# Graph-masked attention on one core: where the softmax probabilities are turned, and which queue places the head halves

## What is computed

```python
h = relu(layernorm(x))                        # x: (32, 256, 384) float32
q, k, v = h @ Wq + bq, h @ Wk + bk, h @ Wv + bv      # 6 heads of 64
scores = einsum('bhqd,bhkd->bhqk', q, k) / 8
bias = where(adj, 0.0, -9e15)[:, None]        # adj: (32, 256, 256) bool
probs = softmax(scores + bias, axis=-1)
ctx = einsum('bhqk,bhkd->bhqd', probs, v)     # back to (32, 256, 384)
out = x + (ctx @ Wf + bf)
```

## Time and profile before

| | us |
|---|---|
| median of three runs | 701.88 (701.35 to 702.62) |
| span of the profiled execution | 701.6 |
| TensorE busy | 677.3 |
| VectorE busy | 555.2 |
| ScalarE busy | 464.9 |
| GpSimd busy | 270.1 |

### The profile page before, as it was taken

How to read it: one execution, slowest core, us unless ns; L and a number is a source line. 1 busy time by engine, 2 the same in 40 slices (tenths; PEclk the granted TensorE clock), 3 DMA queues, 4 the chain that set the end, 5 groups by cost and what they waited for, 6 DMA issues and landing times.

```text
span 701.6 us, 21244 instructions
## 1 busy us (share of the span) xinstructions
PE 677.3 (97%) x7156; PEld 562.7 (80%) x7156; DVE 555.2 (79%) x1676; ACT 464.9 (66%) x972; POOL 270.1 (39%) x330
## 2 busy tenths in 40 slices
PE   7688999999999999999999999999999999999996
PEld 5466888888888888888888888888888888888874
DVE  5748887887887878788787878878787887888785
ACT  2545676767677676767767676776767677676763
POOL 1334444334444433444443344444334444333420
PEclk8899999999999999999999999999999999999998
DMA  5123333433332343333234333323433332343220
GB/s 187 43 52 89 101 72 89 105 85 90 90 98 71 90 105 84 90 92 96 71 91 105 84 87 94 90 74 94 105 81 89 95 88 75 95 105 78 65 71 35
DMA packets 72453, 61.36 MB, mean 87 GB/s; under 512 B 17649, under 2 KB 72434, under 8 KB 72434
## 3 DMA queue, kind: packets, MB, share of 16 engines
q1 hardware_dynamic: 72434, 61.12, 33.8%
HBM read 17.05 MB, written 12.58 MB: 42 GB/s over the span
## 4 chain that ended last, share of the span: by engine, by line
PE 90%; issue 3%; DVE 3%; DMA 1%; ACT 1%; POOL 1%; SPq 0%; POOLq 0%; DVEq 0%
PE ring L767 17%; PE ring L769 17%; PE ring L768 17%; PE probs_t L834 11%; PE scores L824 6%; PE scores L825 6%; PE ctx L850 3%; PE ctx L852 3%; PE ctx L851 3%; PE ring L779 3%; PE ring L860 3%; DMA w_raw<-in_L_gnn_Wv_dram 1%; ACT probs L404 0%; DMA x_in<-in_x_dram 0%; DVE w_lo L623 0%
## 5 line engine op out<-in xcount | busy, mean ns | idle before, releaser
L404 ACT ACTIVATE probs<-logits,least 128x256 f32<-128x256 f32 x384 | 175.1, 504 | 78.0 <-DVE least L536 77.0
L354 POOL TENSOR_TENSOR split<-qk,split 128x512 f16<-128x512 f32 x96 | 111.3, 1160 | 274.9 <-DVE split L559 274.9
L409 ACT ACTIVATE pt_hi<-probs_t 128x512 f16<-128x512 f32 x192 | 114.6, 597 | 108.1 <-PE probs_t L834 107.3
L536 DVE CUSTOM_DVE_ANT_0 logits<-scores,mask,logit_unscale 128x256 f32<-128x256 f32 x384 | 169.1, 478 | 4.5 <-PE scores L825 3.7
L767 PE MATMUL ring<-h_hi,w_hi 128*128 128x256 f16 x576 | 158.3, 275 | 2.0 <-DVE w_lo L623 1.5
L768 PE MATMUL ring<-h_lo,w_hi 128*128 128x256 f16 x576 | 158.1, 275 | 0.0
L769 PE MATMUL ring<-h_hi,w_lo 128*128 128x256 f16 x576 | 158.0, 274 | 0.0
L543 DVE SCALAR_TENSOR_TENSOR pt_lo<-probs_t,pt_hi 128x512 f16<-128x512 f32 x192 | 131.6, 686 | 0.7 <-ACT pt_hi L409 0.6
L834 PE MATMUL probs_t<-ident,probs 128*128 128x128 f32 x768 | 116.4, 274 | 5.4 <-ACT probs L404 5.3
L559 DVE CAST split<-qk 128x512 f16<-128x512 f32 x96 | 41.3, 430 | 98.3 <-ACT qk L422 98.3
L422 ACT ACTIVATE qk<-ring,qk_bias_s,qkv_ratio 128x256 f32<-128x256 f32 x192 | 96.7, 552 | 15.2 <-PE ring L769 15.2
(11 more groups left out here) (86 smaller groups left out, 1300.0 us busy)
## 6 DMA issues: line engine op xcount, KB each, us to landing
heads<-split SPq DMA_DIRECT2D x192, 96.0 KB, 2.2
x_in<-in_x_dram SPq DMA_DIRECT2D x32, 384.0 KB, 3.3
heads<-split SPq DMA_DIRECT2D x192, 64.0 KB, 2.1
out_dram<-result SPq DMA_DIRECT2D x64, 192.0 KB, 1.9
adj_in<-in_adj_dram SPq DMA_DIRECT2D x32, 64.0 KB, 2.0
w_raw<-in_L_gnn_Wq_dram SPq DMA_DIRECT2D x1, 576.0 KB, 4.1
w_raw<-in_L_gnn_Wk_dram SPq DMA_DIRECT2D x1, 576.0 KB, 6.5
w_raw<-in_L_gnn_Wv_dram SPq DMA_DIRECT2D x1, 576.0 KB, 6.3
```

The lines of the kernel that those rows point to most:

```text
L404: act.activation(probs[u % 2][:, a], logits[u % 2][:, a], ACT.Exp, bias=least[u % 2][:, a:a + 1], scale=-1.0).then_inc(probs_ready, 1)
L536: dve.tensor_tensor_reduce(out=logits[u % 2][:, a], in0=score_bank[u % 2][:, a * S:(a + 1) * S], in1=mask[b.parity][:, t], scale=logit_uns ...
```

## The change

Units 0 and 3 (`PE_UNITS`) are turned by TensorE as before, with one PSUM bank for it. The other four are split before they are turned, and turned by DMA:

- `exps` adds ln(2^14) to `least` first (`raised`, a ScalarE operation of 128x2 that the exponentials wait for), so that the probabilities come out scaled. There are three buffers of logits and probabilities in place of two.
- `probs_hi` casts the whole unit on ScalarE into `p_rows[u][:, 0]`, `probs_lo` subtracts on GpSimd into `p_rows[u][:, 1]`; `transpose_probs` on SP then issues one transposing DMA of 128 rows x 1024 float16 (eight blocks of 128x128) into `p_cols[u]`.
- `apply_probs` comes four units after the scores (`LAG`) in place of two.
- `place_heads` on SP keeps the two DMAs that stay on their partitions; the two that cross are issued by ScalarE, `cross_heads`.
- x and the residual have four buffers; the loop body has four batches; h has two buffers; the ring of PSUM banks has four in place of three, and the order of projections, output and splits within a turn is written anew. The second token tile's output is projected one turn later.

```diff
+PE_UNITS = (0, 3)
+RING = 4
+    LAG = 4
-        x_in = [sb(f"x_in{p}", [P, QT, H], F32) for p in range(2)]
+        x_in = [sb(f"x_in{p}", [P, QT, H], F32) for p in range(RING)]
             def place_heads(b, j):
...
                     sp.dma_start(dst[own], src[own, 1:4]).then_inc(heads_placed[j], 16)
-                    sp.dma_start(dst[other, 0:2], src[own, 0:3:2]).then_inc(heads_placed[j], 16)
+            def transpose_probs(b, u):
+                if u in PE_UNITS:
+                    return
+                wait(sp, p_lo_ready, b.count(len(DMA_UNITS), nth_dma(u)))
+                alone(sp)
+                sp.dma_start_transpose(p_cols[u][:].rearrange("p w a s q -> p (w a s) q"),
+                                       p_rows[u][:].rearrange("p w a k -> p (w a k)")).then_inc(p_placed[u], 16)
...
+            def probs_lo(b, u):
+                if u in PE_UNITS:
+                    return
+                wait(pool, p_hi_ready, b.count(len(DMA_UNITS), nth_dma(u)))
+                pool.tensor_tensor(p_rows[u][:, 1], probs[u % 3][:], p_rows[u][:, 0],
+                                   ALU.subtract).then_inc(p_lo_ready, 1)
...
             def exps(b, u):
+                wait(act, logits_ready, b.count(2 * UNITS, 2 * u + 2))
+                alone(act)
+                act.activation(raised[u % 3][:], least[u % 3][:], ACT.Identity,
+                               bias=p_raise[:, 0:1]).then_inc(raised_ready, 1)
+                wait(act, raised_ready, b.count(UNITS, u + 1))
                 for a in range(2):
-                    wait(act, logits_ready, b.count(2 * UNITS, 2 * u + a + 1))
-                    act.activation(probs[u % 2][:, a], logits[u % 2][:, a], ACT.Exp,
-                                   bias=least[u % 2][:, a:a + 1], scale=-1.0).then_inc(probs_ready, 1)
+                    act.activation(probs[u % 3][:, a], logits[u % 3][:, a], ACT.Exp,
+                                   bias=raised[u % 3][:, a:a + 1], scale=-1.0).then_inc(probs_ready, 1)
...
+                wait(act, probs_ready, b.count(2 * UNITS, 2 * u + 2))
+                act.activation(p_rows[u][:, 0], probs[u % 3][:], ACT.Copy).then_inc(p_hi_ready, 1)
...
+            def cross_heads(b, j):
+                wait(act, qk_lo_ready, b.count(C, j + 1))
+                alone(act)
+                for a in range(2):
+                    own, other = slice(D * a, D * a + D), slice(D - D * a, 2 * D - D * a)
+                    dst, src = heads[b.parity][:, 2 * j + a], split[j]
+                    act.dma_start(dst[other, 0:2], src[own, 0:3:2]).then_inc(heads_crossed[j], 16)
...
             def scores(b, u):
                 t, j = u // C, u % C
                 if t == 0:
-                    wait(pe, heads_placed[j], b.count(4 * 16, 4 * 16))
+                    wait(pe, heads_placed[j], b.count(2 * 16, 2 * 16))
+                    wait(pe, heads_crossed[j], b.count(2 * 16, 2 * 16))
...
             def apply_probs(b, u):
                 t, j = u // C, u % C
-                wait(pe, pt_lo_ready, b.count(UNITS, u + 1))
+                if u in PE_UNITS:
+                    wait(pe, pt_lo_ready, b.count(len(PE_UNITS), nth_pe(u)))
+                else:
+                    wait(pe, p_placed[u], b.count(16, 16))
...
+                def attend(u):
+                    if here:
+                        scores(b, u)
+                    if u < LAG:
+                        if before:
+                            apply_probs(b + -1, UNITS - LAG + u)
                     elif here:
+                        apply_probs(b, u - LAG)
+                    if here and u - 1 in PE_UNITS:
                         transpose_probs(b, u - 1)
```

More of the change, by code:

```diff
@@ L56, in gnn_attention @@
     UNITS = QT * C
+    DMA_UNITS = [u for u in range(UNITS) if u not in PE_UNITS]
+    LAG = 4
     assert D * 2 == P and QT == 2 and C == 3 and B % 2 == 0
@@ L119, in gnn_attention @@
         v_lo = [sb(f"v_lo{p}", [P, QT, HEADS, D], F16) for p in range(2)]
[L121 to L125, removed]
+        logits = [sb(f"logits{u}", [P, 2, S], F32) for u in range(3)]
+        least = [sb(f"least{u}", [P, 2], F32) for u in range(3)]
+        raised = [sb(f"raised{u}", [P, 2], F32) for u in range(3)]
+        probs = [sb(f"probs{u}", [P, 2, S], F32) for u in range(3)]
+        p_rows = [sb(f"p_rows{u}", [P, 2, 2, S], F16) for u in range(UNITS)]
+        p_cols = [sb(f"p_cols{u}", [P, 2, 2, QT, P], F16) for u in range(UNITS)]
         inv_sum = [sb(f"inv_sum{t}", [P, HEADS], F32) for t in range(QT)]
@@ L495, in cycle @@
                     weights_hi(3)
-                hi_of(4)
+                if front:
+                    qk_full(b + 1, 2)
                 if here:
                     exps(b, 4)
+                    probs_hi(b, 3)
                 if front:
-                    qk_full(b + 1, 2)
-                    if not first:
-                        v_hi_part(b + 1, 0)
-                hi_of(5)
+                    cross_heads(b + 1, 0)
+                if here:
+                    probs_hi(b, 4)
+                if front:
+                    cross_heads(b + 1, 1)
+                if before:
+                    context_hi(b + -1, 1)
                 if here:
@@ L531, in mask_and_max @@
                     wait(dve, mask_ready, b.count(2, 2))
+                wait(dve, probs_ready, b.count(2 * UNITS, 2 * u - 4))
                 alone(dve)
@@ L588, in finish, with layer_stats @@
                 dve.scalar_tensor_tensor(out=result[t][:], in0=R_OUT[t][:, 0:H], scalar=out_unscale[:, 0:1],
-                                         in1=residual[b.parity][:, t], op0=ALU.mult,
+                                         in1=residual[b.slot][:, t], op0=ALU.mult,
                                          op1=ALU.add).then_inc(result_ready, 1)
-            def layer_stats(b):
-                wait(dve, x_loaded[b.parity], b.dma_count())
-                for t in range(QT):
-                    dve.bn_stats(out=stats[:, t], in_=x_in[b.parity][:, t]).then_inc(moments, 1)
+            def layer_stats(b, parts):
+                if 0 in parts:
+                    wait(dve, x_loaded[b.slot], b.dma_count(RING))
+                for t in parts:
+                    dve.bn_stats(out=stats[:, t], in_=x_in[b.slot][:, t]).then_inc(moments, 1)
+                if 1 not in parts:
+                    return
                 for t in range(QT):
@@ new lines, in cycle @@
+                attend(1)
+                if front:
+                    project_qk(b + 1, 0)
+                attend(2)
+                if before:
+                    transpose_context(b + -1, 0)
+                if front:
+                    project_qk(b + 1, 1)
+                attend(3)
+                if front:
+                    project_qk(b + 1, 2)
+                if b.k == 0:
+                    pe.wait_ge(bf_ready, 1)
+                attend(4)
+                if b.k == 1:
+                    pe.wait_ge(w_lo_ready, 10)
@@ L949, in cycle @@
[L949 to L965 removed]
+                if front:
+                    project_v(b + 1, 0, (1, 2))
+                    project_v(b + 1, 1)
```

389 lines of the change are left out of this document (195 added, 194 removed).

## The result

The changed kernel takes 715.3 us in the median of three runs (710.9 to 720.1), the kernel before 701.8: 1.019 times the time, 95% interval 1.013 to 1.024. That is slower, if by less than 2.5%, where I had forecast 658 us.

The account below looks back on a forecast made before the run. TensorE, busy throughout the loop, was taken as the bound: 20.50 us a turn less 1.76, plus 0.3 for near misses, gives 19.05; 30 turns plus 86.1 us of start and end make 658 us, range 646 to 740.

Parts of the forecast that it names:

- TensorE's floor: TensorE, each turn: 16 of 24 probability transposes go, 1.76 us off 20.50, leaving a floor of 18.74 us.
- The timetable's near misses: Hand-laid turn: 0.2 to 0.7 us slack in four places, 0.8 at pair 2's crossing halves; 0.3 us added, 19.05 a turn.
- The transposing DMA: Probability transposes on the DMA engines: 2.2 us of all engines each, 4.2 us issue to landing, DMA share 0.85, covered.
- ScalarE: ScalarE, each turn: six `raised` at 0.37 us and six DMA issues at 0.62 bring it to 18.0 us, 20.2 if uncovered.
- VectorE's wait for x in the first turn: First turn: VectorE's 4.93 us wait for x of batch 2 goes with four x buffers, -4.9 us.
- The end: Last unit: waits for GpSimd subtraction and DMA instead, +3.9 us, less 0.5 for shorter work; `raised` adds about 1.
- The rivals: Takeover by ScalarE (686 us, chance 0.22), DMA engines (758, 0.12), SP's issue (836, 0.04), or blocks one after another (1620, 0.03).
- The DMA engines' rival: DMA engines become the bound: transposes at 3.8 us each, 22.4 us a turn, 758 us in all; chance 0.12.
- my table of slacks: Hand-laid timetable of a turn: 0.8 us of slack for pair 2's crossing halves, landing at 5.3 us, wanted at 6.1.

Follow-up runs that it names:

- e9: The changed kernel, its loop of four turns kept, with ScalarE issuing pair 2's crossing DMAs at the head of its turn: 684.6 us, ratio 0.973.
- e6: The changed kernel with its loop written out and ScalarE issuing pair 2's crossing DMAs at the head of its turn: 671.5 us, ratio 0.955.
- e10: The changed kernel written out, pair 2's crossing DMAs at the head of ScalarE's turn, GpSimd's pair 2 split before its first-turn reduction: 661.4 us, ratio 0.940.
- e1: The changed kernel with its loop written out, all turns in a row, nothing else different: 711.4 us, ratio 1.010.
- e11: The kernel before, with ScalarE issuing pair 2's crossing DMAs behind the exponentials of unit 0, no DMA transposes: 703.8 us, ratio 1.001.
- E4: The kernel before with four turns in its loop body in place of two, nothing else: 743.2 us, ratio 1.057.
- e3: The changed kernel, with SP holding unit 5's transposing DMA until pair 2's crossing halves have landed: 698.0 us, ratio 0.993.
- e8: The changed kernel written out, GpSimd's pair 2 split before its first-turn reduction, unit 5's transpose held until pair 2's crossing halves land: 680.4 us, ratio 0.967.

## Why the prediction was wrong

By the ratios, the changed kernel loses 4.5 points to the place of two DMA issues (to e9), 1.8 to the jump of the long loop body (e9 to e6), and 1.5 to GpSimd's order in the first turn (e6 to e10): 1.019, 0.973, 0.955, 0.940. The shares depend on the order: with the loop written out first (e1), it brings 0.9 and the place 5.5. The last kernel, 661.4 us, comes near the forecast of 658, in part by luck: within its span the 30 turns take 3.6 us less than forecast (567.9 against 571.5) and all outside them 5.5 us more (91.6 against 86.1).

- **TensorE's floor, right.** 18.74 forecast; the turns of e6 and e10 in which TensorE waits for nothing take 18.88 to 18.89 (567.87 / 30 = 18.93 in the mean of e10). The work that I took off was the work that went.
- **The timetable's near misses, the step that failed.** I had the crossing halves issued up to 3.9 us into the turn, the last from 3.2, landing 2.1 us after the earlier trace rows, 0.8 us before unit 2 wants them, "right while two transposes are under way", and put 0.3 us on all such places. Issue was at 3.5, landing took 3.4 (4.1 in e1), and the place alone cost 0.8 us a turn, 1.2 once the jump's stalls were out of the way. The 2.1 us is a row of a kernel whose DMA engines stand at 0.38 where heads are placed, and whose loop fetches next to no code. I carried it into one that I had myself just filled. The row was right for e11 (2.2) and wrong for the kernel in question. Unit 5's transpose beside them makes it 3.35, an instruction fetch 3.71, both terms that the timetable did not have. A slack should have been weighed against the spread of landings beside other traffic: 0.8 us against a landing 1.3 to 2.0 us longer is no near miss but a wait in almost every turn.
- **The jump back, not in the sum at all.** The loop body of four turns stands in the change, and the prediction puts it at nothing without a reason. E4 prices it at 6.8 us a jump for a TensorE without slack. With the changed kernel's five jumps, e9 against e6 gives 13.1 / 5 = 2.6 us a jump. The longer code also brings the fetches that run on beside the crossing halves.
- **The transposing DMA, right or a little high.** Issue to landing 3.2 us in the median, 4.2 forecast; SP's issue 1.24 us, within 0.4 to 5.0. In e10 the DMA share over 30 turns is 0.76 of 18.93 us, 14.4 us; without the 7.2 us of before, 1.8 us of all engines for each of four, against 2.2. The mean over a turn was below the 0.85 I called covered, but it is not spread evenly: 0.97 for 5.4 us just where the slack was least. The Trainium skill's page DMA: Bandwidth & Descriptors, Latency and other measured facts, made it 1.0 us by its 261 GB/s; the trace has more, the 1.8 us just worked out. The Trainium skill's page VectorE: DVE Perf Modes, The three transpose paths, has 1309 ns for one 128x128 block, and the trace has 3.2 us from issue to landing for eight.
- **ScalarE, right.** `raised` 0.29 us against 0.37, its DMA issue 0.63 against 0.62. It never became the bound (465.70 / 30 = 15.5 us of its busy time a turn in e10).
- **VectorE's wait for x in the first turn, a stall that changed its name.** The 4.9 us did go from VectorE, and I noted "0 if another stall takes its place". One did: GpSimd's reduction and `add_bias` now stand ahead of the split of pair 2. Chain of waits of the changed kernel in the first turn:

```profile
37.28 7.68 issue
44.96 1.94 POOL residual L424 x2
46.90 1.12 POOL split L415
...
48.60 2.43 DMA heads<-split
```

  I costed the new order of GpSimd in a turn as covered, and did not walk the first turn, where that queue holds a wait for other engines. Even e10 takes 61.2 us to turn 1, no less than the kernel before's 60.6.
- **The end, right.** From the last turn's scores on it takes 30.8 us, 25.9 before: +4.9 against +4.4.
- **The rivals.** None was what happened. The DMA engines' rival was about their total over a turn; what decided was what ran on them in one stretch. The sign of the result was in my table of slacks, in the one entry of 0.8 us.

What stays open: why the first stall's removal (e1) left the turn at 20.44 although the jump's waits were gone. That both shared one slack is argued from the waits that grew from 0.81 to 1.19, not shown by a run of its own. The part of the fetches is read from which turns wait in the traces; the changed kernel with a loop body so short that nothing is fetched anew was not tried, and neither was holding both unit 4's and unit 5's transposes.

## What to carry to other kernels

When a change fills a resource, don't time the transfers that stay by rows from when it was empty: look for the least slack in the timetable, and ask what else is on the DMA engines in just those microseconds, instruction fetches included. The first remedy to try for a transfer that lands late is to issue it earlier in the queue it is in, before moving it to another queue or holding back its neighbours. And look at what a change does on the side, the length of the loop body and the order in the first turn: here these two cost as much as 3.3 points, and neither is in the idea of the change.

## What the runs showed of the hardware

- A jump back over a body of two turns took TensorE 0.21 us, over one of four turns 3.8 to 5.2 us, in either kernel. The same kernel written out fetched nearly as much (57 against 74 packets) and waited for nothing at those places.
- A pause of TensorE costs twice: behind the 4.2 us at a jump, the next turn was granted 0.92 of the clock in the mean and took 22.15 us in place of 20.50.
- A DMA can be late though the DMA engines have room in the mean: in e3 a crossing DMA of pair 2 landed in 2.15 us in the median of 13 turns and in 3.81 in the 14 turns in which a 16 KB instruction packet started beside it. In e8 the same two medians are 2.35 and 3.72 us.
- A cast on VectorE doubled in length when it began inside a subtraction on GpSimd. The cast of q and k to float16, all 96 of it, before and after (ns min/median/max):

```profile
L559 DVE CAST split<-qk x96: 416/427/725, 23.1 to 672.4; 128x512 f16<-128x512 f32 x96
```

```profile
L669 DVE CAST split<-qk x96: 416/846/1403, 23.1 to 673.1; 128x512 f16<-128x512 f32 x96
```

  In the changed kernel's trace, 51 of the 96 begin while GpSimd's subtraction into `p_rows` runs, with over 0.15 us of it to go. Each of the 51 ends 0.28 us behind the end of the subtraction, however early it began, and takes 861 ns in the median; 43 of the other 45 take 425 ns or less. Standing beside GpSimd is not enough: in e10, 30 casts begin 0.5 us into a subtraction and take 0.93 us, and 29 begin 0.19 us ahead of one and take 0.42, while that subtraction takes 1.25 us in place of 1.16. So the one that began first went first. VectorE had room for the delay here. This is read from the traces; no run was made for it.
